# Routing's table of token and scale by slot: 64 indirect transfers into DRAM in place of a one-hot product on TensorE

## The reference, cut to what matters

```python
x = x + tanh(g_xattn) * attention(layernorm(x), ctx, ctx, mask)
xt = layernorm(x).reshape(T, D)                      # T = 2048 tokens
scores = softmax(xt @ Wg.T)                          # 16 experts in 4 groups
topi = top_k(scores masked to the 2 best groups, 4)  # 4 experts for each token
combine[t, topi] = scores[t, topi]
y = sum_e combine[:, e] * ((silu(xt @ W1[e].T) * (xt @ W3[e].T)) @ W2[e].T)
z = (silu(xt @ Ws1.T) * (xt @ Ws3.T)) @ Ws2.T        # the shared expert, 704 wide
x = x + tanh(g_ffn) * (y + z)
```

## Time and profile before

| | |
|---|---|
| median of 3 runs | 1240.26 us (1237.85 to 1240.94) |
| the profiled execution's own time | 1240.24 us |
| its span, first to last instruction | 1238.2 us |
| TensorE's mean granted clock | 0.985 |
| busy in the span: PE, DVE, ACT, POOL | 97%, 51%, 47%, 51% |
| shared expert and routing | from about 462 to 664 us of the span |

### The profile page before, as it was taken

One profiled execution on the slowest core, in us unless ns is written; L12 is line 12 of the kernel. 1 busy time (PEld: TensorE's weight loads), 2 busy tenths in 40 slices (PEclk: granted clock), 3 DMA queues, 4 the chain that ended last, 5 costly groups with the idle time before them and its releaser, 6 DMA issues. The chain is left out here.

```text
span 1238.2 us, 23635 instructions
## 1 busy us (share of the span) xinstructions
PE 1199.9 (97%) x7811; PEld 919.4 (74%) x7812; DVE 636.2 (51%) x1832; ACT 576.4 (47%) x990; POOL 626.3 (51%) x662
## 2 busy tenths in 40 slices
PE   7999999999999989999998999999999999999994
PEld 5564555555543458888887999999999999999994
DVE  5337999999965658865142133322523444542100
ACT  1221777777742234322332554555554554555552
POOL 7010333433334124635562666666666667767663
PEclk8999999999989999999999999999999999999997
DMA  9462544444545050100133455665655666665433
GB/s 348 149 189 99 154 125 131 126 135 126 145 134 155 30 204 17 52 35 35 51 121 113 107 102 144 142 150 138 155 138 129 163 147 146 142 150 138 83 61 42
DMA packets 73965, 153.27 MB, mean 124 GB/s; under 512 B 10740, under 2 KB 16372, under 8 KB 73128
## 3 DMA queue, kind: packets, MB, share of 16 engines
q1 hardware_dynamic: 52856, 102.50, 25.6%
q0 software_dynamic: 21040, 49.88, 19.5%
HBM read 97.69 MB, written 52.23 MB: 121 GB/s over the span
## 5 line engine op out<-in xcount | busy, mean ns | idle before, releaser
L1553 DVE CAST e_w<-e_w 128x480 fp32r<-128x480 f32 x135 | 75.7, 561 | 303.9 <-DMA e_w<-in_w2T 299.7
L653 DVE CUSTOM_DVE_ANT_0 a_mb<-a_mb,late 128x512 f32<-128x512 f32 (+1 forms) x480 | 217.3, 527 | 6.3 <-PE a_mb L696 4.6
L1706 PE MATMUL e_yps<-e_w,e_hT 128*128 x711 | 197.2, 404 | 0.9 <-ACT e_hT L1616 0.9
L639 ACT ACTIVATE a_at<-a_eb 128x1024 f32<-128x1024 f32 (+1 forms) x192 | 163.4, 869 | 38.5 <-PE a_eb L717 25.7
L566 POOL TENSOR_SCALAR_AFFINE_SELECT a_at<-a_at 128x256 f32<-128x256 f32 (+1 forms) x192 | 94.2, 491 | 170.6 <-ACT a_at L639 170.6
L1685 PE MATMUL e_up<-e_w,e_xT 128*128 x948 | 170.4, 328 | 0.0
L1685 PE MATMUL e_gate<-e_w,e_xT 128*128 x948 | 169.2, 327 | 1.0 <-issue 1.0
L1685 PEld LDWEIGHTS e_gate<-e_w,e_xT 128*128 128x128 f32 x948 | 157.2, 190 | 11.4 <-issue 6.6
L1685 PEld LDWEIGHTS e_up<-e_w,e_xT 128*128 128x128 f32 x948 | 149.4, 188 | 0.0
L1706 PEld LDWEIGHTS e_yps<-e_w,e_hT 128*128 128x128 f32 x711 | 128.1, 189 | 25.4 <-issue 1.2
L1577 POOL DMA_INDIRECT out<-e_y,scatter x79 | 128.3, 1625 | 25.3 <-issue 14.1
(11 more groups left out here) (265 smaller groups left out, 1873.7 us busy)
## 6 DMA issues: line engine op xcount, KB each, us to landing
e_w<-in_w13T SPq DMA_DIRECT2D x16, 1408.0 KB
dq<-p_parts SPq DMA_DIRECT2D x32, 256.0 KB, 2.4
a_q<-dq SPq DMA_DIRECT2D x64, 128.0 KB
do<-a_o SPq DMA_DIRECT2D x32, 256.0 KB, 2.3
e_w<-in_w2T SPq DMA_DIRECT2D x16, 512.0 KB
a_k<-dk SPq DMA_DIRECT2D x64, 98.0 KB
e_w<-in_ctxT SPq DMA_DIRECT2D x4, 1024.0 KB, 14.1
e_w<-in_x SPq DMA_DIRECT2D x4, 1024.0 KB, 13.5
```

The source lines that it names most:

```text
L639: eng.activation(to, scores, ACT.Exp, scale=0.25).then_inc(s_exp, 1)
L653: eng.tensor_tensor_reduce(out=b[:, 0:w], in0=b[:, 0:w], in1=io["late"][:, SEQ - w:SEQ], scale=1.0, scalar=3 * NEG, op0=ALU.add, op1=ALU.m ...
L1706: mm = eng.matmul(yps[:], hT[r][0:size, mine, n, :], w[0:size, bass.ds(buf, 1), its * SIDE + at:its * SIDE + at + D].rearrange("p b n -> p ...
```

## The change

The product is dropped, and the table is built in DRAM. SP first writes a blank table (the spare row and scale 0 for each of the 79 x 128 slots). DVE turns each pair's slot into a place in this table. Then, for each of 16 groups of tokens and each of 4 choices, GpSimd issues one indirect transfer that writes 128 entries of 8 bytes (token and scale) to their places. All 64 go out in the second and third batch: one between the product and the subtraction of each unit but the last, two behind each subtraction, four behind each `add`, until none is left. In the fourth batch SP waits for all of them and reads the table back; DVE copies `scatter`, `gather` and `scale` out of it. The first four gathers move from ahead of unit 20 to ahead of unit 21. At the first unit of the second batch GpSimd now waits until the blank table is stored and DVE has written the places.

```diff
             eng.wait_ge(s_i, 6)
-            eng.tensor_copy(pad[:], pad_i[:]).then_inc(s_v, 1)
...
-            eng.tensor_copy(tok[:], tok_i[:]).then_inc(s_v, 1)
+            eng.tensor_copy(puti[:, :, :, 0], rows(tok_i[:].rearrange("p (t o) -> p t o", o=1), NK)).then_inc(s_v, 1)
...
-            eng.tensor_copy(iota_p[:], iota_pi).then_inc(s_v, 1)
...
-            eng.tensor_tensor(put[:, :, :, 0], rows(tok[:].rearrange("p (t o) -> p t o", o=1), NK), row[:], ALU.subtract).then_inc(s_v, 1)
-            eng.wait_ge(s_v, next(done))
-            for t in range(NT):
-                r = t % 2
-                if t >= 2:
-                    eng.wait_ge(s_tok, t)
-                eng.tensor_tensor(at_row[r], iota_p[:].rearrange("p (o n) -> p o n", o=1).broadcast_to([P, NK, P]),
...
-                eng.tensor_tensor(at_tile[:], iota_g[:].rearrange("p (o g) -> p o g", o=1).broadcast_to([P, NK, TILES]),
...
-                for n in range(2):
-                    eng.tensor_tensor(at_col[r][:, :, n, :], at_tile[:],
-                                      put[:, t, :, n:n + 1].broadcast_to([P, NK, TILES]), ALU.mult).then_inc(s_row, 1)
+            eng.tensor_scalar(row[:], row[:], float(TILES), None, ALU.mult).then_inc(s_v, 1)
+            eng.wait_ge(s_v, next(done))
+            eng.tensor_tensor(row[:], row[:], col[:], ALU.add).then_inc(s_v, 1)
+            eng.wait_ge(s_v, next(done))
+            eng.tensor_copy(place[:], row[:]).then_inc(s_v, 1)
+            placed.append(next(done))
+            eng.wait_ge(s_v, placed[0])
...
-            eng.wait_ge(s_tok, NT + 1)
-            eng.tensor_scalar(indexf[:], tokps[:, 0:TILES], pad[:, 0:1], None, ALU.add).then_inc(s_v, 1)
-            eng.wait_ge(s_v, next(done))
-            eng.tensor_copy(io["scatter"], indexf[:]).then_inc(s_v, 1)
-            eng.wait_ge(s_v, next(done))
-            eng.tensor_scalar(indexf[:], indexf[:], float(T - 1), None, ALU.min).then_inc(s_v, 1)
-            eng.wait_ge(s_v, next(done))
-            eng.tensor_copy(io["gather"], indexf[:]).then_inc(s_v, 1)
+            eng.wait_ge(s_table, 16)
+            eng.tensor_copy(io["scatter"], index).then_inc(s_v, 1)
+            eng.wait_ge(s_v, next(done))
+            eng.tensor_scalar(io["gather"], index, T - 1, None, ALU.min).then_inc(s_v, 1)
             compared.append(next(done))
             eng.wait_ge(s_v, compared[1])
-            eng.tensor_copy(io["scale"], tokps[:, TILES:]).then_inc(s_v, 1)
+            eng.tensor_copy(io["scale"], table[:, :, 1]).then_inc(s_v, 1)
...
+            entries = itertools.product(range(NT), range(NK))
+
+            def enter(count):
+
+                for t, k in itertools.islice(entries, count):
+                    eng.indirect_dma_start(out=dram["table"], out_offset=bass.IndirectOffsetOnAxis(ap=place[:, t, k:k + 1], axis=0),
+                                           in_=put[:, t, k, :], in_offset=None).then_inc(s_entry, 16)
+
             for i, (b, n) in enumerate(units):
                 size = SCH[n][1]
-                if i == (BATCH - 1) * NS + 2:
+                listed = 0 < b < BATCH - 1
+                if i == NS:
+                    eng.wait_ge(s_blank, 16)
+                    eng.wait_ge(s_v, placed[0])
+                if i == (BATCH - 1) * NS + 3:
                     eng.wait_ge(s_v, compared[1])
                     eng.wait_ge(io["s_xTout"][BATCH - 2], 32)
                     for g in range(XB):
...
                 eng.tensor_tensor(raw[i % 2][0:size], act[i % 2][0:size], upc[i % 2][0:size], ALU.mult).then_inc(s_raw, 1)
+                if listed and n != order[-1]:
+                    enter(1)
                 eng.wait_ge(s_hhigh, i + 2)
                 eng.tensor_tensor(h[0:size, 1, n, :], raw[i % 2][0:size], h[0:size, 0, n, :].bitcast(F32), ALU.subtract).then_inc(s_hlow, 1)
+                if listed:
+                    enter(2)
                 if n == order[-1]:
                     for j in range(CH):
                         if b * CH + j < NT - 1:
                             add(b, j)
+                        if listed:
+                            enter(4)
                         if j == 0 and b + 1 < BATCH:
                             low_x(b + 1)
...
-            def table(t):
-                r = t % 2
-                eng.wait_ge(s_row, 3 * t + 4)
-                for k in range(NK):
-                    mm = eng.matmul(tokps[:], at_row[r][:, k, :], at_col[r][:, k].rearrange("p n g -> p (n g)"), start=t == 0 and k == 0,
-                                    stop=t == NT - 1 and k == NK - 1, skip_group_check=True)
-                mm.then_inc(s_tok, 1)
...
-                if NS + 2 <= i < NS + 2 + NT // 2:
-                    for t in range(2 * (i - NS - 2), 2 * (i - NS - 2) + 2):
-                        table(t)
...
             eng.dma_start(gf[:], io["gf"].broadcast_to([P, 1])).then_inc(s_g, 16)
+            eng.wait_ge(s_i, 6)
+            eng.dma_start(dram["table"].rearrange("(p g) w -> p g w", p=P), table[:]).then_inc(s_blank, 16)
             for b in range(BATCH):
                 if b == BATCH - 1:
+                    eng.wait_ge(s_entry, 16 * NT * NK)
+                    eng.dma_start(table[:], dram["table"].rearrange("(p g) w -> p g w", p=P)).then_inc(s_table, 16)
                     eng.wait_ge(io["s_base"], 16 * CH * b)
                     eng.wait_ge(s_v, compared[0])
                     load_first(eng, io, 0, 0)
```

More of the change, by code:

```diff
@@ L1077, in stage_shared @@
         iota_i, tok_i, iotag_i = sb("r_iotai", [P, E], I32), sb("r_toki", [P, NT], I32), sb("r_iotagi", [P, TILES], I32)
-        tok, slots = sb("r_tok", [P, NT]), sb("r_slots", [P, NT, NK], I32)
-        iota_p = sb("r_iotap", [P, P])
-        iota_pi = iota_p[:].bitcast(I32)
+        slots = sb("r_slots", [P, NT, NK], I32)
         rowi, coli = sb("r_rowi", [P, NT, NK], I32), sb("r_coli", [P, NT, NK], I32)
         row, col = sb("r_row", [P, NT, NK]), sb("r_col", [P, NT, NK])
-        at_row = [io["rows"][2 + r].rearrange("p (k n) -> p k n", k=NK) for r in range(2)]
-        at_tile = sb("r_attile", [P, NK, TILES])
-        at_col = [sb(f"r_atcol{r}", [P, NK, 2, TILES]) for r in range(2)]
         put = sb("r_put", [P, NT, NK, 2])
-        pad_i, pad = sb("r_padi", [P, 1], I32), sb("r_pad", [P, 1])
-        indexf = sb("r_indexf", [P, TILES])
+        puti, place = put[:].bitcast(I32), sb("r_place", [P, NT, NK], I32)
+        table = sb("r_table", [P, TILES, 2])
+        index = table[:].bitcast(I32)[:, :, 0]
         tile_e, tile_b = sb("r_tilee", [1, TILES]), sb("r_tileb", [1, TILES])
         cmp = io["wo"][0:1].rearrange("p k d -> p (k d)")[:, 0:TILES * E].rearrange("p (g e) -> p g e", g=TILES)
-        compared = []
+        compared, placed = [], []
         ps = lambda n, s: c.enter_context(nc.psum_tensor(n, s, F32))
@@ L1094, in stage_shared @@
         within, totals = counts[:, 0], counts[:, 1]
-        tokps = ps("r_tokps", [P, 2 * TILES])
         s_c, s_i, s_exp, s_ch, s_mm, s_v = (
@@ L1098, in stage_shared @@
         ready, expert = sb("r_ready", [1, TILES], I32), sb("r_expert", [1, TILES], I32)
-        s_row, s_tile, s_tok = sem("r_srow"), sem("r_stile"), sem("r_stok")
+        s_blank, s_entry, s_table = dsem("r_sblank"), dsem("r_sentry"), dsem("r_stable")
         weights = shared_weights(io)
@@ L1121, in _ @@
         def _(eng):
-            begin(eng, s_c, s_ch, s_v, s_row, s_tile, s_high, s_low)
+            begin(eng, s_c, s_ch, s_v, s_high, s_low)
             done = itertools.count(2)
             eng.wait_ge(s_i, 6)
-            eng.tensor_copy(pad[:], pad_i[:]).then_inc(s_v, 1)
-            eng.wait_ge(s_v, next(done))
             eng.tensor_copy(iota_e[:], iota_i[:]).then_inc(s_v, 1)
             eng.wait_ge(s_v, next(done))
-            eng.tensor_copy(tok[:], tok_i[:]).then_inc(s_v, 1)
+            eng.tensor_copy(puti[:, :, :, 0], rows(tok_i[:].rearrange("p (t o) -> p t o", o=1), NK)).then_inc(s_v, 1)
             eng.wait_ge(s_v, next(done))
             eng.tensor_copy(iota_g[:], iotag_i[:]).then_inc(s_v, 1)
-            eng.wait_ge(s_v, next(done))
-            eng.tensor_copy(iota_p[:], iota_pi).then_inc(s_v, 1)
             eng.wait_ge(s_v, next(done))
@@ L1352, in _ @@
             eng.iota(iota_i[:], pattern=[[1, E]], base=0, channel_multiplier=0).then_inc(s_i, 1)
-            eng.iota(tok_i[:], pattern=[[P, NT]], base=-T, channel_multiplier=1).then_inc(s_i, 1)
+            eng.iota(tok_i[:], pattern=[[P, NT]], base=0, channel_multiplier=1).then_inc(s_i, 1)
             eng.iota(iotag_i[:], pattern=[[1, TILES]], base=0, channel_multiplier=0).then_inc(s_i, 1)
-            eng.iota(iota_pi, pattern=[[1, P]], base=0, channel_multiplier=0).then_inc(s_i, 1)
-            eng.iota(pad_i[:], pattern=[[0, 1]], base=T, channel_multiplier=1).then_inc(s_i, 1)
+            eng.memset(table[:, :, 1], 0.0).then_inc(s_i, 1)
+            eng.iota(index, pattern=[[0, TILES]], base=T, channel_multiplier=1).then_inc(s_i, 1)
```

(4 more changed lines are left out.)

5 lines of the change are left out of this document (removed).

## The result

The changed kernel takes 1267.72 us (median of 4, 1266.6 to 1268.62) against 1240.6 us before (median of 4, 1237.85 to 1241.05): 1.0227 times as long, with an interval from 1.0208 to 1.0246. The forecast was 1260 us, range 1246 to 1288: right in direction and range, 7.7 us short in size. The profiled execution took 1266.6 us, its span is 1264.9 us.

What follows compares the result with a forecast made beforehand. TensorE was taken as the bound, with GpSimd becoming it through the entries: fourth batch starts 21.3 us late, its down ends 18.1 late, plus 1.6 for the clock, 19.7 us on 1240.26: 1260 us, range 1246 to 1288.

Steps and rivals of the forecast that it cites:

- TensorE bounds, and gives back 17.4 us: Second and third batch: TensorE sets the pace before the change; eight dropped pairs at 2.18 us free 17.4 us.
- The price of an entry, 0.99 us by the gather's row: Each of the 64 indirect transfers holds GpSimd 0.99 us, as a gather does; 0.9 to 1.2 us given 0.70.
- A (0.52): Entries cost a small direct transfer's 0.52 us, TensorE stays the bound: 1235 us, or 1223 at no price; chance 0.10.
- B (1.60): Each entry holds GpSimd as long as the adding scatter, 1.60 us: 38 us on top, 1298 us; chance 0.10.
- The number of addresses: Reason for the entry's price: the same 128 addresses as in the gather, and bytes are not what is paid for.
- GpSimd paces the two batches: Second and third batch take GpSimd's time, 66.3 and 63.7 us, 130.0 in all, against TensorE's 45.8 each.
- Where GpSimd paces, a slow TensorE costs nothing: A lowered TensorE clock was taken to cost no time wherever GpSimd sets the pace.
- The clock term: Last down product, fourth batch: TensorE's lower clock behind a wait loses 1.6 us, bounds 0 and 16.
- the 3 forecast: Fourth batch: TensorE was to wait 3 us for GpSimd's low part ahead of the last down product.
- The fourth batch gives back 3 us: Without entries the fourth batch recovers a little: 21.3 us late at its first product, 18.1 at its down's end.
- The table is read back in time: Fourth batch: table read back and copied by 650.2, 3 us ahead of unit 21's need, so hidden.
- rival C: Entries land slowly, at 2.5 us each in the queue; gathers start 25 us later: 1285 us; chance 0.05.
- The experts' stage ... starts as much later: Behind the fourth batch: the experts' stage is untouched and only shifts by the delay before it.

Runs made afterwards that it cites:

- the first of the four: Against the changed kernel, VectorE takes GpSimd's vector work of the second and third batch; GpSimd only issues the 64 entries in a row: 1288.12 us, 1.0375.
- the first kernel in which GpSimd kept the products: Against the kernel where VectorE took the vector work: GpSimd keeps products, three entries behind each, four behind each of ScalarE's parts: 1233.85 us, 0.9954.

## Why the prediction was right, and where it fell short

- **TensorE bounds, and gives back 17.4 us.** Right: without entries 18 us less than before.
- **The price of an entry, 0.99 us by the gather's row.** Right: 0.95 to 1.09. Rivals A (0.52) and B (1.60) are out. The number of addresses, part of the reason given, hardly matters: half of them save 6%, so the price was met partly by luck. By the Trainium skill's "DMA: Bandwidth & Descriptors", section "Anatomy of one DMA — SWDGE (gpsimd) path", most of a transfer's fixed cost is the receipt of the written data. In this trace GpSimd doesn't wait for that: the next entry starts 0.30 us behind the last one's end.
- **GpSimd paces the two batches.** Right; the run with both product and entries shows it from the other side. The forecast of 130.0 us became 649.59 - 512.74 = 136.85.
- **"Where GpSimd paces, a slow TensorE costs nothing"** is the step that failed. TensorE's down waits for GpSimd's low part, so it starts late and, behind that wait, at the lower clock for some 6 us; and GpSimd's first add waits for that down. It came 11.0 and 10.6 us behind the down's start, for 8.2 in the second batch of the kernel before and for 8.2 in both batches with TensorE kept busy. This took 2.90 + 2.45 us of GpSimd's time. The clock term was put on the last down, which ran at 16.23 us, behind a wait of 0.47 instead of the 3 forecast. Keeping TensorE busy took 4.3 us off the time and both waits away. The first product of the second batch, 2.51 us for the usual 1.28, is another 1.2 us. It runs beside VectorE's first two comparisons; in the three kernels in which GpSimd keeps the products and VectorE has its comparisons later, it takes 1.28 or 1.29 us. No run changed that alone.
- **The fourth batch gives back 3 us.** It gave 2.9: from first product to last down 22.78 us, against 647.58 - 621.94 = 25.64 before.
- **The table is read back in time.** Right: no wait, so rival C is out.
- **"The experts' stage ... starts as much later."** Short by 2.45 us. From the last down's end to the first transposes it is 693.76 - 688.60 = 5.16 us, before 666.40 - 663.69 = 2.71 (the down's end by the earlier trace rows). What holds them is the memset of `e_h`, and ahead of it the DRAIN of GpSimd's queue, which the prediction put at nothing.

The sum: 6.4 us later into the fourth batch than forecast (5.35 + 1.2, the start 0.5 earlier, the rest in units of 6.23 for 6.17 and rounding), 0.3 us less made good in it, 1.5 us less for the last down's clock, 2.45 us at the stage's end, and an experts' stage 0.7 us shorter: 7.0 us, which is the span's 26.7 us more in place of 19.7.

## What to carry to other kernels

Work that is moved to an idle engine is paid by the place it gets in that engine's order: with the same 64 transfers the change costs 27 us or gains 14, by where they stand in GpSimd's list and by what else it has to do there. Sum the receiving engine's time for each unit of the pacing engine, not over the stage, and where the pace changes hands follow each wait once around: an engine that has become idle may start late, at a lower clock, and hold up the new bound.

## What the runs showed of the hardware

- **Close rows of indirect transfers hold up the other engines.** In the four kernels in which VectorE has all the vector work and 16 or more entries follow in a row, most at one in 1.27 us, ScalarE begins to wait after 13 or 14 of them (2.2, 3.6, 5.1 and 4.4 us ahead of its next instruction). Where the row goes on, TensorE comes nearly to a stand after 21 to 31. ScalarE goes on 1.0, 8.2, 2.4 and 2.0 us after the row's end. A row of 10 or 12 alone does not do this, nor do three in 5 us over a whole batch. A small instruction behind every fourth entry changes nothing, and the transfers keep up with their issue: from 560 to 590 us of the first of the four the queue moved 736 packets, at 32 an entry those of 23. What the engines share with them is open. In that run the trace has no packet of the instruction queues between 540 and 600 us, which may be a cause or a consequence. The one row of 16 with GpSimd's products around it fell where ScalarE waited for GpSimd anyway, so no run tells whether VectorE's share of the work has a part in it.
- **GpSimd's DRAIN at the end of the stage grows with its entries.** It takes 1.72 us without any (the kernel before, the run without entries), 5.66 us with 48, and 6.96 to 7.26 us in the eleven kernels with 64, with 64 addresses each as with 128, whatever their order. That is (5.66 - 1.72) / 48 = 0.08 us an entry, and (6.96 - 5.66) / 16 = 0.08 again. In those eleven the experts' memset waits 6.11 or 6.12 us for it behind GpSimd's last add. Why it grows, no run shows.
- **Behind a wait TensorE's next product can run at the lower clock.** Behind waits of 4.78 and 7.29 us a down product of 16.1 us took 2.9 and 2.5 us more, behind 9.75 and 7.23 us 12 matmuls of 2.88 us took 1.65 and 2.58 us more, each granted 0.50 or 0.51 at first. The length of the wait does not settle it: in the first kernel in which GpSimd kept the products, a down behind 2.79 us took 18.99 us (0.50 from 588 to 592 us), and 12 matmuls behind 3.27 us took 3.00 (1.00 from 568 to 572 us).
